# Mamba mixer tiles between two mixture-of-experts layers: the last tile's projection in front of M x xdt, B x xw at the tile's end, y summed, gated and transposed in halves

## The reference

```python
x = x + 0.5 * ffn(layernorm(x))      # 8 experts, top 2, and a shared one
x = x + mixer(layernorm(x))
x = x + 0.5 * ffn(layernorm(x))

def mixer(u):
    z, xBC, dt = split(u @ W_in.T)
    x, B, C = split(silu(causal_conv4(xBC) + conv_b))     # 1024, 128, 128
    dt_s = softplus(dt + dt_bias);  dA = exp(-exp(A_log) * dt_s)   # 16 heads
    def step(state, t):              # state: 16 heads x 64 x 128
        state = dA[t] * state + x[t] * (dt_s[t] * B[t])
        return state, state @ C[t]
    y = scan(step) + x * D
    yg = y * silu(z)
    yn = yg * rsqrt(mean(yg * yg) + 1e-5) * norm_w
    return yn @ W_out.T
```

## Time and profile before

| | us |
|---|---|
| median of 3 runs | 1641.28 (1639.50 to 1648.27) |
| the profiled execution | 1640.93 |
| its span, first to last instruction | 1639.2 |
| PE busy in the span | 1524.5 (93%) |
| DVE, ACT, POOL busy | 1048.6, 750.1, 795.7 |
| mean granted TensorE clock | 0.976 of full |

### The profile page before, as it was taken

The page is one execution under the profiler, slowest core; times in us unless marked ns, Lnnn a source line. Parts: engine busy times, 40 slices in busy tenths (PEclk is TensorE's granted clock), DMA queues, the critical chain, the costliest instruction groups (busy, mean ns, idle before and its releaser), DMA issues. The chain is left out here.

```text
span 1639.2 us, 23899 instructions
## 1 busy us (share of the span) xinstructions
PE 1524.5 (93%) x8530; PEld 1294.4 (79%) x8530; DVE 1048.6 (64%) x1739; ACT 750.1 (46%) x1290; POOL 795.7 (49%) x475
## 2 busy tenths in 40 slices
PE   6989999999999989998888899889889999999999
PEld 6767999999877777786667778668668999999877
DVE  7664565666467876687558767765673656566465
ACT  4211666666413653454245346434212666666411
POOL 2111777766444545535524553552111777766442
PEclk9989999999999999999889999997989999999999
DMA  7032677777352110020012002014122778777244
GB/s 287 27 106 63 238 271 265 262 256 273 120 181 78 65 65 1 27 79 12 0 51 68 1 23 69 1 36 148 45 88 79 252 256 280 250 266 280 84 155 128
DMA packets 70872, 214.42 MB, mean 131 GB/s; under 512 B 8096, under 2 KB 8096, under 8 KB 69856
## 3 DMA queue, kind: packets, MB, share of 16 engines
q1 hardware_dynamic: 48672, 155.18, 26.9%
q0 software_dynamic: 11360, 37.23, 7.6%
q10 hardware_dynamic: 10720, 20.45, 3.4%
HBM read 179.80 MB, written 33.03 MB: 130 GB/s over the span
## 5 line engine op out<-in xcount | busy, mean ns | idle before, releaser
L626 POOL TENSOR_TENSOR g_lo<-g_raw,g_hi 128x1408 fp32r<-128x1408 f32 x54 | 179.4, 3322 | 260.9 <-ACT g_hi L753 260.6
L626 POOL TENSOR_TENSOR u_lo<-u_raw,u_hi 128x1408 fp32r<-128x1408 f32 x54 | 174.2, 3226 | 67.8 <-ACT u_hi L753 67.8
L1671 PE MATMUL bank<-u_hi,xgT 128*128 128x352 f32 x624 | 168.5, 333 | 0.0
L1671 PE MATMUL bank<-g_hi,xgT 128*128 128x352 f32 x624 | 162.7, 323 | 0.0
L1694 PE MATMUL bank<-d_hi,hT 128*128 128x512 f32 (+1 forms) x468 | 159.7, 395 | 1.8 <-DVE hT L1054 1.8
L691 POOL TENSOR_TENSOR w_hl<-w_raw,w_hl 128x1024 fp32r<-128x1024 f32 x36 | 88.9, 2470 | 139.9 <-ACT w_hl L753 139.9
L1623 PE MATMUL bank<-xs,g_hi 128*128 128x512 f32 (+1 forms) x384 | 130.4, 422 | 7.5 <-DVE gate L1200 6.6
L1639 PE MATMUL bank<-d_hi,hT 128*128 128x512 f32 (+1 forms) x384 | 126.2, 402 | 5.8 <-DVE hT L1054 3.5
L801 ACT ACTIVATE gate<-bank 128x512 f32<-128x512 f32 (+1 forms) x48 | 28.6, 596 | 222.5 <-PE bank L1623 214.8
L1054 DVE TENSOR_TENSOR hT<-bank,hT 128x384 fp32r<-128x384 f32 x78 | 43.1, 552 | 128.9 <-ACT hT L753 128.9
L1385 DVE SCALAR_TENSOR_TENSOR acc<-pre,cw,acc 128x512 f32<-128x512 f32 x120 | 121.7, 1015 | 4.3
(11 more groups left out here) (255 smaller groups left out, 3688.7 us busy)
## 6 DMA issues: line engine op xcount, KB each, us to landing
g_raw<-in_w_gate SPq DMA_DIRECT2D x54, 704.0 KB, 5.6
u_raw<-in_w_up SPq DMA_DIRECT2D x54, 704.0 KB, 6.5
d_raw<-in_w_down SPq DMA_DIRECT2D x54, 512.0 KB, 5.0
w_raw<-in_w_in SPq DMA_DIRECT2D x37, 512.0 KB, 3.2
routed_y<-ys ACTq DMA_DIRECT2D x32, 512.0 KB, 4.7
d_raw<-in_w_down SPq DMA_DIRECT2D x54, 192.0 KB, 5.4
token_x<-xn SPq DMA_DIRECT2D x8, 1024.0 KB, 5.3
X<-in_x SPq DMA_DIRECT2D x4, 1024.0 KB, 10.3
```

The source lines that it names most:

```text
L626: pool.tensor_tensor(half_of(piece, 1, s), raw_at[piece][s % RING][:], half_of(piece, 0, s).bitcast(F), ALU.subtract)\
L1671: ins = pe.matmul(dst[:, 0:FE], xgT[:, n % 2, hx, kc], half_of(piece, hw, NS + j)[:, kc], start=(m == 0), stop=(m == 3 * KD - 1))
```

## The change

The last tile's y is now transposed in two halves at the very front of a tile, around decays 0 and 1. The x transposes are split too. C x S comes before decays 3, the projection of the last tile follows, then the transposes of acc, then M x xdt, and B x xw is last. On DVE the groups of M are spread: M 0 in front of xD, M 1 and M 2 behind the scaling into y, then the scaling of acc (l_xn), then M 3. The sum of y is done in halves, each after its half of M x xdt, with the residual between them; the state's sum is last. POOL gates y in halves and does `rms` and the rsqrt ahead of xw. ACT does the squares and the copy of G and B between L 1 and L 2. Semaphores m_yi, m_yg and m_E count halves.

```diff
 # POOL, in a tile
-    pool.wait_ge(l_var, i * TPB + (n + TB + 1))
-    rsqrt_ln(slice(q, q + 1), l_rstd)
     ...  # S[:, (n + 1) % 2] = S[:, n % 2] * dec, m_Sd
+    pool.wait_ge(l_var, i * TPB + (n + TB + 1))
+    rsqrt_ln(slice(q, q + 1), l_rstd)
+    if q >= 1:
+        rms(n - 1)
     ...  # xw = xdt * wd, m_xw
-    if q >= 1:
-        rms(n - 1)
     after(m_yc, n + 1, TPB)
     after(m_xD, n + 1, TPB)
     pool.tensor_tensor(y[:, n % 2], y[:, n % 2], xD[:], ALU.add).then_inc(m_yd, 1)
-    after(m_yi, n + 1, TPB)
-    pool.tensor_tensor(y[:, n % 2], y[:, n % 2], zs[:, q], ALU.mult).then_inc(m_yg, 1)
+    for half in range(2):
+        hs = slice(half * DI // 2, (half + 1) * DI // 2)
+        after(m_yi, 2 * n + half + 1, 2 * TPB)
+        pool.tensor_tensor(y[:, n % 2, hs], y[:, n % 2, hs], zs[:, q, hs], ALU.mult)\
+            .then_inc(m_yg, 1)
 # ACT, for g in range(HG), before the exponentials of group g
+    if g < 2 and q >= 1:
+        y_hi(n - 1, (g,))
+    if g == 2:
+        if q >= 1:
+            squares(n - 1)
+        after(m_G, n + 1, TPB)
+        ...
+        act.activation(GB[:], bank[3][:, 0:2 * P], ACT.Copy).then_inc(m_Bt, 1)
 # DVE, the new order of a tile
+    if q >= 1:
+        y_lo(n - 1)
+    ln_stats([x_next], [q], l_var)
+    after(m_xt, 2 * n + 2, 2 * TPB)
+    ...
+    halves(xdt, of_heads(dts, q * HEADS), 4, m_xdt)
+    after(m_Bt, n + 1, TPB)
+    decayed(0)
+    after(m_yd, n, TPB)
+    halves(xD, of_heads(hp, 2 * HEADS), 4, m_xD)
+    after(m_C, n + 1, TPB)
+    ...
+    halves(y[:, n % 2], of_heads(ecs, q * HEADS), 6, m_yc)
+    decayed(1)
+    decayed(2)
+    dve.wait_ge(l_rstd, i * TPB + (n + TB + 1))
+    dve.wait_ge(l_tp, i * TPB + (n + TB - 1))
+    ln_scale(xn_m[:, q % 2], x_next, q).then_inc(l_xn, 1)
+    decayed(3)
+    ...  # low part of xb
+    after(m_yd, n + 1, TPB)
+    y_add(0)
+    if q >= 1:
+        residual(n - 1)
+    y_add(1)
+    ...  # S += bank 4, 5
+def decayed(g):
+    after(m_L, HG * n + g + 1, HG * TPB)
+    dve.tensor_tensor(L[:, g * GH:(g + 1) * GH], L[:, g * GH:(g + 1) * GH],
+                      some(GB[:, 0:P], GH), ALU.mult).then_inc(m_M, 1)
+def y_add(half):
+    hs = slice(half * DI // 2, (half + 1) * DI // 2)
+    after(m_E, 2 * n + half + 1, 2 * TPB)
+    dve.tensor_tensor(y[:, n % 2, hs], y[:, n % 2, hs], bank[6 + half][:], ALU.add)\
+        .then_inc(m_yi, 1)
 # PE, in a tile
+    if q >= 1:
+        y_features(n - 1, (0,))
     decays(n, q, 0)
     decays(n, q, 1)
+    if q >= 1:
+        y_features(n - 1, (1,))
+    after(m_S, n, TPB)
+    x_rows(0)
     ...  # G and B
     decays(n, q, 2)
-    if q >= 1:
-        y_features(n - 1)
-    decays(n, q, 3)
-    if q >= 1:
-        project(n - 1)
+    x_rows(1)
     ...  # C x S, m_C
+    decays(n, q, 3)
+    if q >= 1:
+        project(n - 1)
     ...  # transposes of acc, after l_xn
-    ...  # B x xw, then M x xdt
+    ...  # M x xdt (m_E after each half), then B x xw
```

More of the change, by code:

```diff
@@ L941, in conv_out, with y_hi @@
                         act.activation(xc[:, c], acc[:, c % 2], ACT.Silu).then_inc(m_xc, 1)
-                    def y_hi(n):
-                        for half in range(2):
+                    def y_hi(n, halves=range(2)):
+                        for half in halves:
                             after(m_F, 2 * n + half + 1, 2 * TPB)
@@ L1461, in turn @@
                             x_next = X[:, bass.ds(nxt, 1), :].rearrange("p o n -> p (o n)")
[L1462 to L1474, removed]
@@ L1475, in turn @@
-                            ins.then_inc(m_xdt, 1)
-                            if q >= 1:
[L1477 to L1492, removed]
+                            def halves(tile, coefs, width, signal):
+                                for half in range(2):
+                                    hs = slice(half * DI // 2, (half + 1) * DI // 2)
+                                    ins = dve.tensor_tensor(heads_of(tile[:, hs]), heads_of(bank[width + half][:]),
+                                                            each(coefs[half], HD), ALU.mult)
+                                    if half == 0:
+                                        own.mark(ins)
+                                ins.then_inc(signal, 1)
@@ L1493, in turn @@
+                            of_heads = lambda t, at: [t[:, at + half * HB:at + (half + 1) * HB] for half in range(2)]
+                            def decayed(g):
                                 after(m_L, HG * n + g + 1, HG * TPB)
@@ L1808, in turn, with y_features @@
                     after, settle = loop_waits(pe, i)
-                    def y_features(n):
-                        after(m_yg, n + 1, TPB)
-                        for half in range(2):
+                    def y_features(n, halves=range(2)):
+                        for half in halves:
+                            after(m_yg, 2 * n + half + 1, 2 * TPB)
                             for c in range(4):
@@ L1972, in turn @@
                             ins.then_inc(l_tp, 1)
+                            after(m_yc, n + 1, TPB)
+                            for g in range(HG):
+                                after(m_M, HG * n + g + 1, HG * TPB)
+                                for h in range(g * GH, (g + 1) * GH):
+                                    ins = pe.matmul(bank[6 + h // 8][:, (h % 8) * HD:(h % 8 + 1) * HD], L[:, h],
+                                                    xdt[:, h * HD:(h + 1) * HD], start=True, stop=True)
+                                if g % 2:
+                                    ins.then_inc(m_E, 1)
                             after(m_xw, n + 1, TPB)
```

70 lines of the change are left out of this document (21 added, 49 removed).

## The result

The changed kernel takes 1666.76 us (median of 4 runs, 1662.69 to 1672.21), the kernel before 1640.80 (4 runs, 1639.50 to 1648.27). The ratio is 1.016, with an interval of 1.014 to 1.019. Forecast were 1650 us and a range up to 1664: the sign is right, the size is not. The profiled execution took 1664.8 us, span 1663.1, with a mean granted TensorE clock of 0.965 where it was 0.976.

What follows compares the result with a forecast made beforehand. PE, through its waits, was taken to bound the kernel. Later tiles -6.2, first tiles +19.0, their clock +10.4 less 0.6, turn ends -13.7 gave +8.9 on 1640.93, about 1650 us; range 1629 to 1664.

Steps and rivals of the forecast that it cites:

- The bound: Whole kernel: PE is busy 93% of the span, so a change gains only what PE stops waiting for.
- the end of the gate wait and of the yT wait: Later tiles: PE's waits for POOL's gate and yT's low part vanish, 2.17 us a tile, 26 us if that were all.
- the new wait for acc in all 16 tiles: Transposes of acc wait for DVE's scaling, held up by y + xD: 1.6 us in later tiles, 6.2 in first tiles.
- the later tile: Each of 12 later tiles takes 18.55 us instead of 19.07, -6.2 us in all.
- the first tile at full clock: Each of 4 first tiles takes 18.6 us instead of 13.84, +19.0 us in all.
- the turn's end: From the last tile's end to the residual 7.9 us; two turn ends together gain 13.7 us.
- rival A: M 2 and y + xD on DVE and POOL don't exclude each other; the change gains, 1621 us; chance 0.17.
- rival B: The clock holds in the first tiles, so no change, 1640 us; chance 0.15.
- Clock in first tiles: PE falls to half clock behind the long wait, costing 2.6 us in each first tile, +10.4 us (ends 0 and +15.6).
- rival C: Idle 1.6 us before M x xdt lowers the clock in half of 12 later tiles, 2 us each: 1662 us; chance 0.18.

Runs made afterwards that it cites:

- experiment 2: Changed kernel with POOL's y + xD cut to 8 of 1024 columns, the D term of the others left out: 1636.30 us, ratio 0.998.
- Experiment 6: Changed kernel with four unused 512-column matmuls added in first tiles, between the transposes of acc and M x xdt: 1664.54 us, ratio 1.015.
- the second profile: Profile of the changed kernel measured once more without any edit: 1672.26 us, ratio 1.020 to the kernel before.
- Experiments 5 and 7: 5: the changed kernel once more, 1672.26 us, ratio 1.020. 7: changed kernel with POOL's gate as one whole instruction, 1677.16 us, ratio 1.025.
- experiment 3: Changed kernel with the scaling of acc moved directly behind xD, in front of the scaling into y: 1625.27 us, ratio 0.990.
- experiment 1: Changed kernel with six unused matmuls filling PE's wait before the transposes of acc in first tiles: 1645.07 us, ratio 1.004.
- experiment 8: Changed kernel with acc scaled behind xD, scaling into y behind M 1 and M 2, first tiles partly in old order: 1614.58 us, ratio 0.986.
- experiment 4: Changed kernel with first tiles in their old order on all engines, y still summed and gated in halves: 1631.23 us, ratio 0.995.

## Why the prediction was wrong

**What held.** The bound (PE, through its waits), the end of the gate wait and of the yT wait, the new wait for acc in all 16 tiles with its two sizes (1.6 and 6.2 us forecast, the first with the 0.16 of overlap; 1.21 to 1.34 listed and 6.0 to 6.1 measured), the later tile (18.55; 18.56 to 18.68), the first tile at full clock (18.6; 18.7), the turn's end (7.9; 7.97). That the later tile agrees so closely is partly luck: without any wait it takes 17.1 us (experiment 2), not the 16.9 that I worked out, and the wait costs 1.4 to 1.5 with the overlap, not 1.6. M's maximum of 2889 ns, ending with y + xD, and experiment 2 decide against rival A: the two engines exclude each other here. This is what the Trainium skill's page "SBUF — State Buffer", section "Who interferes with whom", states for the pair. The measured clock decides against rival B.

**What failed** is the step "Clock in first tiles": "At half clock a stretch costs half its length: 1.7 to 3.9 us ... I take 2.6 (near the middle)". It measured 5.3 in each. The fall itself was forecast rightly; how long it lasts was not. I read the length of half-clock stretches from 821 and 834, 7.9 and 5.7 us, where most of what follows the wait are 24 and 48 matmuls of 512 columns, and took it over to a place where 32 products of 64 columns follow. There it was 10.1 to 12.1 us behind the wait. Experiment 6 shows that what follows the wait doubles the stretch: 13.7 us with M x xdt first, 6.8 with four wide matmuls ahead of it, and with these the cost is 2.7, the value forecast. Even my upper end, 3.9 each, was below it. The error is 4 x 2.7 = 10.8 us.

**What was only a rival.** I left out of the sum that a wait of some 1.2 us in front of M x xdt can lower the clock in later tiles (rival C, 0.18). It did so in 2 of 12, for 6.6 us, and in 3 in the second profile. C was priced at half of the tiles and 2 us; it was fewer tiles (8 of 72 over all profiles) at 3.3 us. I held against it that two short waits in old tiles never lowered the clock. They stood in front of the y transposes and the projection, the new one stands in front of the transposes of acc and M x xdt; whether that is the reason was not tried.

**What was in no step.** In two first stages the clock fell at a wait for ACT's zs of some 2.7 us, which made 3.6 us. The rows of this wait, two of the kernel before and one of the changed kernel:

```profile
581.80 13.27 PE L1908 MATMUL bank<-w_hl,xs 128*128 128x256 f32 x96 [2.75 <-ACT zs L986]
720.11 11.78 PE L1908 MATMUL bank<-w_hl,xs 128*128 128x256 f32 x96 [2.70 <-ACT zs L986]
...
728.87 14.44 PE L1907 MATMUL bank<-w_hl,xs 128*128 128x256 f32 x96 [2.69 <-ACT zs L989]
```

In the kernel before, the clock fell at one of its four such waits (at 581.80, ahead of the stretch counted above) and stayed up at three. In the changed kernel it fell at three of four, and in the profiles of all nine runs of changed kernels at 25 of 36. The fall was thus there to be seen in the trace before. The wait itself is as long as it was; why it costs the clock more often now is open.

These two kinds of clock loss, 10.2 us, are the rest of the miss in the mixer: 8.9 + 10.8 + 10.2 = 29.9 of 30.8. Either one alone, added to 1650 us, would have stayed inside the range (1661 and 1660); both together give 1671, and the 6.9 us outside the mixer bring the measured time back near 1665.

A slip without effect: the chances by rival add up to 0.18 for faster and 0.33 for the same, not 0.17 and 0.34.

**What stays open.** Why the clock falls at a given wait of 1.2 or 2.7 us and not at its twin a tile or a block away. Experiments 5 and 7 show that the places change between runs and with the kernel. What selects them is not settled.

## What to carry to other kernels

An idle time of PE can cost more than itself, and how much depended here on what follows it: with M x xdt (64 columns) first, 6.0 us of idle time lost 5.3 us more behind it; with four matmuls of 512 columns first, 2.7; at the old turn's end, where the transposes of y and the projection follow 3.8 us, 3.4 (transposes and projection 10.2 us instead of 6.8). When an order is written for a loop, lay it out once for each kind of round; the first tile of a block has no projection that could hide the new chain, and that alone turned a gain into a loss. And on a chain that PE waits for, don't put an instruction with two SBUF inputs on DVE right behind the signal that starts a large POOL instruction: moving the one scaling ahead of that signal was worth 2.6 points.

## What the runs showed of the hardware that I had not expected

- With M x xdt (128x64, fp32) first behind the wait, PE was at 0.50 for 13.7 us in eight of eight first tiles of the changed kernel's two profiles, against 6.8 us in four of four with matmuls of 512 columns first (experiment 6). The Trainium skill's page "TensorE: Matmul & The Clock Gate", section "HAM oscillation — how this bites in real kernels", has the fall in every round, and the trace agrees. That the stretch is longer or shorter by what stands behind the same wait is from these runs.
- Waits far shorter than the 3.8 us of the kernel before were followed by a fall, but not always: 1.2 to 1.3 us in front of the transposes of acc in 8 of 72 later tiles, 2.7 us for zs in 25 of 36 first stages of changed kernels, and 1.9 us in four of four first tiles of experiment 3, with two more short waits at M x xdt.
- More work made the kernel faster (experiment 1, by 1.2 points), and 5.8 us of it in each first tile cost 0.4 (experiment 6).
- In the version of experiment 8 two waits of 1.40 and 0.69 us, 1.1 us apart, were enough for a short fall in three of four first tiles, although the same two in experiment 4 were not in any; in the kernel before, 1.36 and 0.69 us were in one of four (606 to 609.5). One of the three:

```profile
742.00:745.50 3.50, 3.42 (x8) 1.67 (x9) 3.45 (x6) 2.19 (x9) 1.97 (x1) 0.52 0.01 2
```
